# A two-layer graph network on one core: four buffers for merged sums, ScalarE's program written out by group, products of the counts at half size

## The reference, cut to what matters

```python
h = relu(layernorm(x));  x = x + RGCN2(h)          # two relational layers
h = relu(layernorm(x));  x = x + MESSAGES(h)       # one message-passing layer

def _rgcn_layer(x, W, SW, b, src, dst, rel):       # 8 relations
    msg = einsum('nd,rde->rne', x, W)[rel, src]
    agg = segment_sum(msg, dst, num_segments=N)
    return relu(agg + x @ SW + b)
```

## Time and profile before

| | us |
|---|---|
| median of 3 runs (2960.65 to 2963.27) | 2960.8 |
| the profiled execution | 2965.21 |
| its span | 2963.5 |

### The profile page before, as it was taken

One profiled execution on the slowest core, in us unless ns is written; L12 is line 12 of the kernel. 1 busy time (PEld: TensorE's weight loads), 2 busy tenths in 40 slices (PEclk: granted clock), 3 DMA queues, 4 the chain that ended last, 5 costly groups with the idle time before them and its releaser, 6 DMA issues. The chain is left out here.

```text
span 2963.5 us, 56389 instructions
## 1 busy us (share of the span) xinstructions
PE 2203.0 (74%) x16219; PEld 1880.8 (63%) x16219; DVE 2125.7 (72%) x7344; ACT 1585.1 (53%) x3382; POOL 2016.0 (68%) x1479
## 2 busy tenths in 40 slices
PE   4778988888578898888835665677777777566765
PEld 4678988888578898888835554444444444454553
DVE  6878877777333677666628775677777777499999
ACT  5996655555333444444417766444444443467774
POOL 6754777655667288888767773688877776455555
PEclk9999999999889999999978888899998988799998
DMA  7985555555389545555439998345444443466663
GB/s 245 313 287 132 108 103 101 99 86 95 39 319 365 177 86 86 87 87 86 77 66 400 412 409 324 84 85 94 84 91 84 84 91 50 144 192 191 197 197 131
DMA packets 268196, 473.22 MB, mean 160 GB/s; under 512 B 62736, under 2 KB 142288, under 8 KB 268112
## 3 DMA queue, kind: packets, MB, share of 16 engines
q1 hardware_dynamic: 158352, 382.24, 39.4%
q0 software_dynamic: 109760, 90.00, 20.0%
HBM read 291.28 MB, written 180.81 MB: 159 GB/s over the span
## 5 line engine op out<-in xcount | busy, mean ns | idle before, releaser
L1135 POOL DMA_INDIRECT s<-E_summed,c_scat x392 | 654.2, 1669 | 285.8 <-ACT E_summed L1314 164.9
L1363 PE MATMUL ps<-c_w,E_masked 128*128 128x128 f32 x6272 | 722.1, 276 | 3.2 <-DVE E_masked L1166 3.2
L1363 PEld LDWEIGHTS ps<-c_w,E_masked 128*128 128x128 f32 x6272 | 713.6, 193 | 4.0 <-DVE E_masked L1166 4.0
L1166 DVE SCALAR_TENSOR_TENSOR E_masked<-E_type_row,E_hT 128x512 f32<-128x512 int32 x784 | 484.6, 688 | 79.4 <-ACT E_hT L1283 66.9
L366 POOL DMA_INDIRECT E_src_rows<-s,c_src x392 | 414.9, 1058 | 166.5 <-issue 118.0
L1473 POOL DMA_INDIRECT s<-E_summed,c_scat x196 | 320.9, 1637 | 107.9 <-issue 56.4
L366 POOL DMA_INDIRECT E_src_rows<-in_x,c_src x196 | 192.9, 984 | 103.5 <-issue 74.2
L1462 POOL DMA_INDIRECT E_ends<-x,c_near x196 | 198.2, 1011 | 95.7 <-issue 57.3
L1314 ACT COPY E_summed<-ps 128x512 f32<-128x512 f32 x98 | 57.5, 586 | 374.9 <-DMA s<-E_summed,c_scat 374.9
L572 PE MATMUL ps<-c_sl,N_hT 128*128 128x128 f32 x1568 | 199.9, 282 | 18.1 <-DVE N_out L407 13.0
L1378 PE MATMUL ps<-E_msg,E_same 128*128 128x128 bf16 (+1 forms) x2450 | 207.3, 241 | 1.3 <-DVE E_msg L1216 1.3
(11 more groups left out here) (142 smaller groups left out, 4787.5 us busy)
## 6 DMA issues: line engine op xcount, KB each, us to landing
s<-N_out SPq DMA_DIRECT2D x147, 512.0 KB, 4.9
N_xin<-in_x SPq DMA_DIRECT2D x98, 512.0 KB, 13.1
N_sin<-s SPq DMA_DIRECT2D x98, 512.0 KB, 5.6
E_dst_row<-in_dst_line SPq DMA_DIRECT2D x147, 256.0 KB, 4.8
E_type_row<-in_type SPq DMA_DIRECT2D x98, 256.0 KB, 3.9
N_xin<-s SPq DMA_DIRECT2D x49, 512.0 KB, 6.1
x<-N_x SPq DMA_DIRECT2D x49, 512.0 KB, 11.3
N_xin<-x SPq DMA_DIRECT2D x49, 512.0 KB, 4.0
```

What stands on the lines that cost most here:

```text
L1135: pool.indirect_dma_start(s, bass.IndirectOffsetOnAxis(ap=c["scat"][:, k:k + 1], axis=0), summed[:, g % 2, t * D:(t + 1) * D], None, compu ...
L1166: nc.vector.scalar_tensor_tensor(out=masked[:, u % 2, r, :], in0=type_row[:, u, :], scalar=float(r), in1=hT[:, u % 2, :], op0=ALU.is_equal ...
L1363: ins = nc.tensor.matmul(ps[:, 2 + u % 2, t * D:(t + 1) * D], masked[:, u % 2, r, t * P:(t + 1) * P], w[:, r, :], start=(r == 0 and t == 0 ...
```

## The change

`summed` gets four buffers in place of two, so the copy of group g waits for the landing of the scatter of group g-4. ScalarE's program is written out by group in both passes. `before` is kept in bfloat16. `zeros` has one row of 128 columns, and the stores read it five times.

```diff
-    zeros = keep("zeros", [P, DUMP_FOLD * D])
+    zeros = keep("zeros", [P, D])
...
-                sp.dma_start(a[s][NODES:ROWS_S, :].rearrange("(p k) d -> p (k d)", k=DUMP_FOLD),
-                             zeros[:]).then_inc(loaded, 16)
+                sp.dma_start(a[s][NODES:ROWS_S, :].rearrange("(p k) d -> p k d", k=DUMP_FOLD),
+                             each_tile(zeros, DUMP_FOLD)).then_inc(loaded, 16)
...
-    summed = sb(f"{name}_summed", [P, 2, GE])
+    summed = sb(f"{name}_summed", [P, UNROLL, GE])
...
-        before = sb(f"{name}_before", [P, SAME_COLS])
+        before = sb(f"{name}_before", [P, SAME_COLS], BF16)
...
-                        summed[:, g % 2, t * D:(t + 1) * D], None, compute_op=ALU.add).then_inc(added, 16)
+                        summed[:, g % UNROLL, t * D:(t + 1) * D], None, compute_op=ALU.add).then_inc(added, 16)
...
-                wait(act, added, 64 * (g - 1))
-                nc.scalar.copy(summed[:, u % 2, :], ps[:, 4 + u % 2, :]).then_inc(summed_ready, 1)
+                wait(act, added, 64 * (g - 3))
+                nc.scalar.copy(summed[:, u, :], ps[:, 4 + u % 2, :]).then_inc(summed_ready, 1)
...
-            sweep(act, step)
+            unrolled(step)
```

## The result

The changed kernel takes 2966.7 us (median; 2961.05 to 2972.37), the kernel before 2960.1 on the same chip (2954.71 to 2966.18): 1.0023 times as long, interval 1.0013 to 1.0033. So it is 6.6 us slower. The forecast was 2959, slightly faster; the time lies inside the range, on the other side of the old time. The profiled execution of the kernel before was 5 us above its median, that of the changed kernel at it, so the two spans (2963.5 and 2965.1) differ by 1.6 only.

The account below looks back on a forecast made before the run. GpSimd's chain of scatter issues and landing was taken to bound the edge passes. Terms -3 - 4 + 4 - 1 + 1 + 0 + 1 = -2 gave 2963.2 for the profiled execution, 4.4 less as median: 2959, range 2945 to 2971.

Parts of the forecast that it names:

- GpSimd's chain: Both edge passes: four scatter issues, then the landing, set the group time, 11.40 to 11.61 us and 10.72.
- Rivals 1 and 2: First pass faster: copy holds GpSimd, about 2907, chance 0.05; or the lead lasts past gathers' end, 2941, chance 0.10.
- Rival 4: Either pass: loads settle in another place and it takes the other's period, 19 us either way; chance 0.05.
- the signs named: Profile after: GpSimd's wait put down to the landing; copy waits for scatters only from about group 20 in both passes.
- The first pass's laps: First pass: loads drift against scatters for two more laps, some 16 groups at 11.2 us against 11.40, 3 us gained.
- a crossing: First pass: drifting loads meet the end of the scatter issues, a late landing, two groups of about 12.4 us.
- a denser VectorE: Passes: busier VectorE lengthens GpSimd's issues, 0.1 us per group, +2.5 over 28 groups, taken as inside the bounds.
- The first pass's end, -4: First pass: two groups of 11.6 us become groups without loads at 9.64, -4 us (-2 to -6).
- The second pass's drift, +4 (0 to +9): Second pass: drifting takes loads out of a good place, 12 groups at about 11.1 us against 10.72, +4 us.
- Its end: Second pass, last groups: only issues beside a quiet VectorE become shorter, -1 us.
- Zeros, program, products, +1 +1 0: Setup's broadcast zero stores +1 us, fetching ScalarE's longer code in the passes +1, half-size counts' products 0.
- Rival 3: Slower: second pass loses its good place, first pass's laps +2, setup and code 3 each; +12, 2973, chance 0.10.

Follow-up runs that it names:

- 4 MiB: Types and destinations copied into one DRAM tensor, destinations 4 MiB behind the types, in the kernel before and the changed kernel: 2962.5 and 2972.6 us.
- 4 MiB + 4 KiB: Types and destinations copied into one DRAM tensor, 4 MiB and 4 KiB apart, in the kernel before and the changed kernel: 2942.8 and 2951.4 us.
- the added wait: SyncE's row loads also wait for the scatters' landing six groups earlier; arrays 4 MiB + 4 KiB apart: kernel before 2915.7 us, changed kernel 2917.0.

## Why the prediction was wrong, point by point

- **GpSimd's chain is the bound, the copy's wait is slack: right.** Waits of the copy fell by a third and a fifth, the time rose; with the landings cleared it fell by 27 us with two buffers. Rivals 1 and 2 are out: groups 21 to 38 of the changed kernel's first pass take (709.05 - 504.15)/18 = 11.38 us. Rival 4 is out as well: once the copy waits, the loads are issued 3.2 to 4.0 us before the end of the scatter issues in the first pass (3.1 to 4.6 before) and 4.7 to 5.4 in the second (4.8 to 5.4 before). Two of the signs named failed: GpSimd's wait is still put down to the copy, and in the second pass the copy waits from group 15 on, not 20.
- **The first pass's laps: the step that failed.** Once the copy waits, the loads keep their place in every group: call these groups locked. The forecast took 16 drifting groups at 11.2 us on the mean against locked ones at 11.40, and so a gain of 3 (bounds -8 to +2). Measured over groups 7 to 20: a loss of 3.0 in the two first profiles, (504.15 - 341.31) - (500.02 - 340.16), which is 11.63 us a group against 11.42; of 3.0 with 4 MiB, of 6.7 with 4 MiB + 4 KiB. The first scatter of group 21 of the kernel before, and of groups 7, 11 and 13 of the changed one:

```profile
500.02 1.67 POOL L1135 DMA_INDIRECT s<-E_summed,c_scat  x1 [0.39 <-ACT E_summed L1314]
```

```profile
341.31 1.61 POOL L1135 DMA_INDIRECT s<-E_summed,c_scat  x1 [2.59 <-DMA s<-E_summed,c_scat]
...
385.51 2.13 POOL L1135 DMA_INDIRECT s<-E_summed,c_scat  x1 [0.30 <-issue]
...
410.85 1.61 POOL L1135 DMA_INDIRECT s<-E_summed,c_scat  x1 [2.05 <-DMA s<-E_summed,c_scat]
```

The number of laps was right, and a crossing, groups 11 and 12, takes 25.3 us where two groups of 12.4 were forecast. The waits went the way forecast: over these groups GpSimd is idle for 1.6 us less, 1.7 less with 4 MiB and 1.4 less with 4 MiB + 4 KiB, half of the gain of 3. What failed is the term beside it, GpSimd's own issues. The forecast built its groups from scatter issues of 1.689 us and gathers of 1.017, gave 0.1 us per group to a denser VectorE, an estimate of 2.5 in all, and left that out of the sum as inside the bounds. By line, groups 7 to 20 before (340.16 to 500.0) and changed (341.31 to 504.1):

```profile
L1135 POOL DMA_INDIRECT s<-E_summed,c_scat x56 | 96.6, 1725 | 26.5 <-ACT E_summed L1314 13.4 <-issue 13.1
L366 POOL DMA_INDIRECT E_src_rows<-in_x,c_src x28 | 28.6, 1022 | 8.5 <-issue 8.5
```

```profile
L1135 POOL DMA_INDIRECT s<-E_summed,c_scat x56 | 98.1, 1752 | 26.3 <-issue 14.9 <-DMA s<-E_summed,c_scat 6.2 <-ACT E_summed L1314 3.3
L366 POOL DMA_INDIRECT E_src_rows<-in_x,c_src x28 | 31.7, 1131 | 8.5 <-issue 8.2 <-DMA s<-E_summed,c_scat 0.3
```

Issues and gathers take 4.6 us more (4.7 with 4 MiB, 8.1 with 4 MiB + 4 KiB), 0.3 to 0.6 per group instead of 0.1, and that makes the loss. So the groups that are clear of the loads, 7 to 10 and 13 to 15, take 11.0 us on the mean and not 10.6 to 10.9. What lengthens the issues stays open: VectorE is busy for 0.86 of this stretch instead of 0.76, as the forecast's estimate would have it, but with the added wait the issues are as long (1.766 and 1.077 us) with VectorE at 0.81.
- **The first pass's end, -4: too much.** Groups 39 to 47 gain 1.5 us at 4 MiB + 4 KiB and 1.7 at 4 MiB. With the 4 KiB the two groups that are freed of loads took 11.4 and 10.1 us, not 11.6, and take 10.0 and 10.1 now. The 4.1 that the two first profiles showed there, and 4.0 more in groups 21 to 38, came with loads that landed 0.1 and 0.2 us sooner (4.1 and 4.9 against 4.2 and 5.1). The agreement of -6.9 with -7 was luck: with the distance fixed the pass is 4.0 to 4.7 us longer. How much of the -6.9 is the arrays' place, and how much that the profiled execution of the kernel before lay 5 us above its median, no run tells.
- **The second pass's drift, +4 (0 to +9): right, at the upper half.** Groups 7 to 20 cost +8.0 in the two first profiles, +6.8 and +4.5 with fixed distances. GpSimd's idle time is 4.0, 3.8 and 2.8 of these, longer issues and gathers the rest; the plainest crossing is 1093.70 to 1107.25, 13.55 us. Its end gained 1.4 to 2.0 for the 1 forecast.
- **Zeros, program, products, +1 +1 0: right within what shows.** The first cast starts at 9.87 (10.5 forecast, 9.60 in the earlier trace rows); VectorE's widest count takes 742 ns as in the earlier trace rows, now with a half-size output. Of the gain from full unrolling that the Trainium skill (Runtime: NRT & Kernel Launch, Instruction fetch mechanics) lets one expect, nothing shows beyond the intervals: 2939.6 us with the program written out and two buffers, 2942.8 with the loop.

```profile
L1178 DVE SCALAR_TENSOR_TENSOR E_before<-E_dst_row,c_dstf,c_earlier 128x512 bf16<-128x512 int32 x49 | 36.4, 742 | 0.0
```

- **Rival 3, slower by the drift in both passes, is what happened** in kind. Of its +12, 6 were for setup and code, which cost nothing that shows; +8.6 and +10.0 were measured, more than the 6 that it leaves to the passes, and in the first pass by longer issues, which it does not name. What the forecast did not have at all is that two programs with the same first pass differ by 20 us there. The +6.6 of the changed kernel (interval 3.8 to 9.8) differs from these two by no more than the intervals; whether the arrays' places gave some of it back isn't shown.

Left open: where the given arrays lie in each program, and what moves them, isn't in the trace. With 4 MiB the locked groups 21 to 39 of the changed kernel are 0.23 us longer each than before's, with 4 MiB + 4 KiB equal; the distance alone doesn't explain that. Of the +15.7 us between the two profiled spans with 4 MiB + 4 KiB, 8.7 lie outside the passes; one of these executions was the fastest of its kernel, 5.0 below its median, the other 2.0 above, so this is put down to the spread, without proof.

## What to carry to other kernels

More buffers for an engine with slack don't speed the chain that it feeds; they let the engine run ahead, and what it triggers, here loads, slides through the places where it delays the chain, while the chain's own instructions can take longer: look at their mean duration in the stretch, not only at the waits. Tie such a transfer to the event that it must not meet. And before a stage's difference between two programs is put down to an edit, see whether a stage that the edit doesn't touch moved too; if it did, fix where the arrays lie, and compare then.

## What the runs showed of the hardware

Two loads that each read one 2 KB line 128 times at the same time depend on the distance of their arrays: 4.4 and 5.0 us from issue to landing 4 MiB apart, 3.8 and 4.5 with 4 KiB more, worth 20 us of 2960. Only these two distances were tried. And 768 KB of loads and stores issued 3 to 4 us before the end of a group's scatter issues made the next group start 0.8 to 2.0 us later than the 2.4 after the last issue (groups 26 to 36 of the kernel before), and not later if they are issued 0.65 us before the group's first scatter (the same groups of the kernel before with 4 MiB + 4 KiB and the added wait). GpSimd's issue of an indirect DMA has no fixed length: over groups 7 to 20 a scatter's took 1.677 us on the mean and a gather's 1.039 with two buffers, 1.770 and 1.143 with four (both with 4 MiB + 4 KiB).
